# A bias row moved from TensorE's accumulation to GpSimd, in a three-layer graph attention kernel

## The reference

```
q = x @ Wq[k].T + bq[k];  kk = x @ Wk[k].T + bk[k]
scores = where(mask, -1e10, q @ kk.T / sqrt(128))
attn = where(mask, 0, softmax(scores))
ctx = (attn @ x) @ Wc[k].T
x = layer_norm(x + ctx, ln_g[k], ln_b[k])      # k = 0, 1
```

## Time and profile before

| | |
|---|---|
| median of 3 runs | 1202.79 us (1202.02 to 1202.92) |
| profiled execution, its own time | 1202.1 us |
| span of its trace | 1200.0 us, granted TensorE clock 0.989 of full |
| TensorE matmul busy | 1154.6 us (96%), 9596 matmuls |
| VectorE busy | 982.9 us (82%) |
| ScalarE busy | 928.5 us (77%) |
| GpSimd busy | 530.9 us (44%) |

### The profile page before, as it was taken

One profiled execution on the slowest core, in us unless ns is written; L12 is line 12 of the kernel. 1 busy time (PEld: TensorE's weight loads), 2 busy tenths in 40 slices (PEclk: granted clock), 3 DMA queues, 4 the chain that ended last, 5 costly groups with the idle time before them and its releaser, 6 DMA issues.

```text
span 1200.0 us, 28462 instructions
## 1 busy us (share of the span) xinstructions
PE 1154.6 (96%) x9596; PEld 843.5 (70%) x9596; DVE 982.9 (82%) x2688; ACT 928.5 (77%) x2115; POOL 530.9 (44%) x398
## 2 busy tenths in 40 slices
PE   7788999999999999999999999999999999999796
PEld 4566677777777777777777777777777777777463
DVE  5777788888888888888888888888888888988776
ACT  4426887888888788888878888887888888788774
POOL 1222445443564444356444534644453464444330
PEclk9898999999999999999999999999999999999999
DMA  8015160532517053251615325261432516122311
GB/s 228 19 36 141 20 190 24 148 81 73 140 37 194 19 141 90 72 141 36 180 33 136 89 72 148 36 179 34 127 89 80 148 36 180 34 71 72 111 32 36
DMA packets 164446, 112.48 MB, mean 94 GB/s; under 512 B 100944, under 2 KB 146000, under 8 KB 164304
## 3 DMA queue, kind: packets, MB, share of 16 engines
q1 hardware_dynamic: 162144, 102.80, 33.1%
q0 software_dynamic: 2160, 7.87, 1.9%
HBM read 61.87 MB, written 25.17 MB: 73 GB/s over the span
## 4 chain that ended last, share of the span: by engine, by line
PE 87%; DVE 6%; issue 2%; ACT 2%; DMA 2%; POOL 1%; DVEq 0%; SPq 0%; POOLq 0%; ACTq 0%
PE ps_j L848 39%; PE ps_t L861 22%; PE ps_j L988 9%; PE ps_s L840 8%; PE ps_s L834 6%; ACT probs L1048 1%; DMA xt<-ys 1%; DVE masked_s L1149 1%; PE ps_j L996 1%; POOL ys L674 1%; PE ps_j L955 0%; DVE wq L1199 0%; DVE y_l L1268 0%; DMA x<-x_dram 0%; DVE stats_L L1169 0%
## 5 line engine op out<-in xcount | busy, mean ns | idle before, releaser
L1149 DVE CUSTOM_DVE_ANT_0 masked_s<-ps_s,mask 128x512 f32<-128x512 f32 x640 | 424.6, 681 | 21.8 <-PE ps_s L840 20.7
L1048 ACT ACTIVATE probs<-masked_s,nm_h 128x512 f32<-128x512 f32 x512 | 367.3, 718 | 70.4 <-DVE nm_h L1149 63.9
L861 PE MATMUL ps_t<-ident,probs 128*128 128x128 f32 x2560 | 391.3, 276 | 5.6 <-ACT pt_h L1054 2.8
L861 PEld LDWEIGHTS ps_t<-ident,probs 128*128 128x128 f32 x2560 | 306.1, 142 | 85.5 <-issue 23.5
L1054 ACT ACTIVATE pt_h<-ps_t 128x512 f32<-128x512 f32 x401 | 236.2, 589 | 79.0 <-PE ps_t L861 74.3
L840 PE MATMUL ps_s<-stack 128*128 128x512 f16 x512 | 194.5, 380 | 2.6 <-DVE nm_h L1149 1.7
L848 PE MATMUL ps_j<-xw,pt_l 128*128 128x256 f16 x1536 | 189.1, 274 | 2.1 <-DVE xw L1294 2.1
L848 PEld LDWEIGHTS ps_j<-xw,pt_l 128*128 128x128 f16 x1536 | 151.0, 98 | 32.9 <-issue 2.2
L656 POOL TENSOR_TENSOR rstd_L<-var_eps_L,minus_half 128x4 f32<-128x4 f32 x32 | 32.8, 1024 | 246.5 <-DVE var_eps_L L1179 246.5
L988 PE MATMUL ps_j<-pt_h,v 128*32 128x256 f32 x2048 | 123.6, 382 | 2.4 <-DVE pt_h L1156 2.4
L1184 DVE TENSOR_TENSOR pt_l<-ps_t,pt_l 128x512 f16<-128x512 f32 x128 | 88.3, 690 | 32.5 <-ACT pt_l L1054 26.1
(11 more groups left out here) (140 smaller groups left out, 1639.4 us busy)
## 6 DMA issues: line engine op xcount, KB each, us to landing
stack<-bounce SPq DMA_DIRECT2D x256, 128.0 KB, 3.1
bounce<-parts SPq DMA_DIRECT2D x64, 256.0 KB, 2.6
adj_t<-adj_dram SPq DMA_DIRECT2D x30, 512.0 KB, 5.2
x<-x_dram SPq DMA_DIRECT2D x16, 512.0 KB, 3.9
out_dram<-y_f POOLq DMA_DIRECT2D x15, 512.0 KB, 3.4
stack<-adj_dram SPq DMA_DIRECT2D x2, 512.0 KB, 5.6
pt_h<-l_wc SPq DMA_DIRECT2D x2, 256.0 KB, 4.6
out_dram<-y_f SPq DMA_DIRECT2D x4, 128.0 KB, 1.8
```

The costliest lines, as they stand in the source:

```text
L861: last = pe.transpose(ps_t[r % 2][:, t], probs[:, r, t * P:(t + 1) * P], ident[:])
L1048: act.activation(probs[:, r], masked_s[:, r], ACT.Exp, bias=nm[:, n, r:r + 1], scale=-1.0, accum_out=total[:, n, r:r + 1]).then_inc(exps, 1)
L1149: dve.tensor_tensor_reduce(out=masked_s[:, r], in0=ps_s[scores_bank(pos)][:], in1=m[:, r], scale=-scale, scalar=NONE_LEFT, op0=ALU.add, op ...
```

## The change

The four bias matmuls of each graph's layer 1 XW job go, and with them `mean_64`. `bx1` is kept as one float32 row on all partitions. A new GpSimd function, `add_bx`, multiplies it by `has_l` (1 or 0 for each node) into a scratch tile (`y_l`, or `y_f` for graphs 0 and 1), four instructions of 128x256, and adds the tile to `x1`, one of 128x1024. VectorE gets one small reduction for each graph's layer 0, which makes `has_l` from the sums. GpSimd's order in a pass becomes `split_o(i, 1)`, `split_x(i+3)`, `add_bx(i+2)`, `finish(i)`, and the two M jobs go from tiles 29 and 32 to 33 and 34.

```diff
@@ LOOP_JOBS
-    ("M", None, "i+3", 0, (29,)),
-    ("M", None, "i+3", 1, (32,)),
+    ("M", None, "i+3", 0, (33,)),
+    ("M", None, "i+3", 1, (34,)),
@@ gpsimd
-                pool.tensor_tensor(dst[:], dst[:], h, ALU.add).then_inc(ln_done[s], 1)
+                pool.tensor_tensor(dst[:], dst[:], h, ALU.add).then_inc(shifted if norm == 0 else ln_done[s], 1)
...
+            def add_bx(b, dst):
+
+                if early(b, 1):
+                    pool.wait_ge(bias_ready, 1)
+                    settle(pool)
+                pool.wait_ge(shifted, b + 1)
+                spread = (y_f if early(b, 2) else y_l)[:]
+                for t in range(NT):
+                    last = pool.tensor_scalar(spread[:, t], bx1[:], zero[:], has_l[:, b % 2, t:t + 1], ALU.add, ALU.mult)
+                last.then_inc(bx_spread, 1)
+                pool.wait_ge(bx_spread, b + 1)
+                last = pool.tensor_tensor(dst[:], dst[:], spread, ALU.add)
+                last.then_inc(ln_done["L"], 1)
...
             layer_norm_l0(0, 0, x1)
+            add_bx(0, x1)
...
                 layer_norm_l0(i + 2, 0, x1)
+                split_o(i, 1)
                 split_x(i + 3)
-                split_o(i, 1)
+                add_bx(i + 2, x1)
                 finish(i)
@@ tensor, job XW
                     if early(b, 1) and l == 1:
-                        pe.wait_ge(bias_ready, 1)
                         pe.wait_ge(weights_ready, 2)
...
-                                             lambda a, c: wc0[:, a, l, c], more=l == 1)
-                        if l == 1:
-                            last = pe.matmul(out_bank[:, t * D:(t + 1) * D], mean_64[:], bx1[:],
-                                             start=False, stop=True)
+                                             lambda a, c: wc0[:, a, l, c])
@@ vector, job B
-                    dve.tensor_scalar(bx1[:], wide[:, 0:D], UP, None, ALU.mult).then_inc(bx1_hi, 1)
-                    dve.wait_ge(bx1_hi, 1)
-                    lower = slice(P // 2, P)
-                    dve.scalar_tensor_tensor(bx1[lower], wide[lower, 0:D], UP, bx1[lower], ALU.mult, ALU.subtract)\
-                        .then_inc(bias_ready, 1)
+                    dve.tensor_copy(bx1[:], wide[:, 0:D]).then_inc(bias_ready, 1)
@@ vector, job AV
+                        if l == 0:
+                            dve.tensor_reduce(has_l[:, b % 2], sum_l[:, sums_buffer(b, l), :, 0:3:2], ALONG, ALU.min)
-                        dve.tensor_reduce(some_l[:], sum_l[:, sums_buffer(b, l)], ALONG, ALU.max).then_inc(some_ready, 1)
+                        dve.tensor_reduce(some_l[:], sum_l[:, sums_buffer(b, l), :, 0:2], ALONG, ALU.max).then_inc(some_ready, 1)
```

More of the change, by code:

```diff
@@ L155, in graph_attention @@
         shift_c = sb("shift_c", [P, 2, DC])
-        bx1 = sb("bx1", [P, D], fp16)
-        mean_64 = sb("mean_64", [P, P], fp16)
+        bx1 = sb("bx1", [P, D])
         bv1 = sb("bv1", [P, D])
@@ L195, in graph_attention @@
         nm_h = sb("nm_h", [P, H, NT])
-        sum_l = sb("sum_l", [P, 2, NT, 2])
+        sum_l = sb("sum_l", [P, 2, NT, 3])
         sum_h = sb("sum_h", [P, H, NT])
         some_l = sb("some_l", [P, NT])
+        has_l = sb("has_l", [P, 2, NT])
+        zero = sb("zero", [P, 1])
         r_l = sb("r_l", [P, NT])
@@ L233, in graph_attention @@
         ident_zero, ident_in, half_in = sem("ident_zero"), sem("ident_in"), sem("half_in")
-        mean_in, bo_added, bx1_hi = sem("mean_in"), sem("bo_added"), sem("bx1_hi")
+        bo_added, shifted, bx_spread = sem("bo_added"), sem("shifted"), sem("bx_spread")
         pt_lo_ready, xw_hi = sem("pt_lo_ready"), sem("xw_hi")
@@ L645, in _ @@
             pool.memset(sum_l[:, :, :, 1:2], SUM_FLOOR).then_inc(floors_in, 1)
+            pool.memset(zero[:], 0.0).then_inc(floors_in, 1)
+            pool.memset(sum_l[:, :, :, 2:3], 1.0).then_inc(floors_in, 1)
             for s in "LF":
                 pool.memset(moments[s][:, :, 2:3], LN_EPS).then_inc(floors_in, 1)
-            pool.memset(mean_64[:], 1.0 / 64).then_inc(mean_in, 1)
             pool.wait_ge(ident_zero, 1)
@@ L760, in _ @@
             pool.tensor_tensor(x1[:], y_f[:], shift[:, 0:1, :].to_broadcast([P, NT, D]), ALU.add)\
-                .then_inc(ln_done["L"], 1)
+                .then_inc(shifted, 1)
+            add_bx(1, x1)
             pool.tensor_tensor(x2[:], y_l[:], gain[:, 1:2, :].to_broadcast([P, NT, D]), ALU.mult)\
@@ L781, in _ @@
             split_o(LOOPS - 1, 1)
+            add_bx(LOOPS + 1, x1)
             finish(LOOPS - 1)
@@ L1034, in _ @@
             pe.wait_ge(ident_in, 1)
-            pe.wait_ge(mean_in, 1)
             program(walk)
@@ L1301, in job @@
                         if early(L, 1):
-                            dve.wait_ge(floors_in, 3)
-                        dve.tensor_reduce(some_l[:], sum_l[:, sums_buffer(b, l)], ALONG, ALU.max).then_inc(some_ready, 1)
+                            dve.wait_ge(floors_in, 5)
+                        if l == 0:
+                            dve.tensor_reduce(has_l[:, b % 2], sum_l[:, sums_buffer(b, l), :, 0:3:2], ALONG, ALU.min)
+                        dve.tensor_reduce(some_l[:], sum_l[:, sums_buffer(b, l), :, 0:2], ALONG, ALU.max).then_inc(some_ready, 1)
                         dve.wait_ge(some_ready, L + 1)
```

## The result

The changed kernel is slower, by little: 1204.4 us in the median of 17 runs (1203.46 to 1206.31) against 1202.02 (1201.03 to 1204.07) for the kernel before, a ratio of 1.0019 (95% interval 1.0011 to 1.0026). I had forecast 1197.4 us and a range from 1195.4 to 1200.4.

The account below looks back on a forecast made before the run. TensorE was taken to bound the loop, and chains across engines the prologue. 6.2 us gained less 0.24 and 0.5 lost gave 5.4 us, so a median of 1197.4 us, range 1195.4 to 1200.4.

Parts of the forecast that it names:

- What bounds the kernel, and the price of the matmuls: Loop: TensorE bounds it, so four matmuls fewer save 0.44 us a pass, 6.2 us in 14 passes.
- The eight matmuls of the prologue: Prologue, graphs 0 and 1: removing them counts as nothing; at full price 0.9 us more.
- What comes on GpSimd: Loop: 4.6 us more GpSimd work a pass, ending 3.8 us before `finish` is due; cost nothing.
- The transfer: Loop: the transposing transfer behind `split_x(i+3)` is issued about 2.5 us later, with nothing waiting; cost nothing.
- The masks: Loop, VectorE: M moved behind a later mask tile costs 0, with bounds of 0 and some 0.2 us a pass.
- small waits: Rival, loop or prologue: TensorE waits 0.1 to 0.3 us a pass, or longer prologue; 1199 to 1201.5 us, chance 0.14.
- The prologue: Before the loop: 0.24 us lost to reductions and 0.5 us to VectorE's `wc` pieces.
- the `wc` pieces: Prologue: two VectorE instructions stand until GpSimd's new work ends at 56.8; 0.5 us, bounds 0 and 2.4.
- the two reductions: Prologue, VectorE: graphs 0 and 1 each pay for the new reduction, 0.12 us apiece, 0.24 us in all.
- Nothing comes of it: another chain is exactly as long: Rival, loop: the 0.44 us a pass turn into waits on another chain; 1202.8 us, chance 0.05.
- M is caught: Rival, loop: GpSimd's addition makes M stand 2.4 us; +1.3 us a pass, 1221 us with the prologue, chance 0.09.

Follow-up runs that it names:

- e10: Kernel before without the 64 bias matmuls, nothing in their place, and with the bank pair at tiles 30 and 32: 1196.08 us, ratio 0.9948.
- e11: Kernel before with the M jobs at tiles 33 and 34 and the bank pair at tiles 30 and 32: 1202.38 us, ratio 0.9999.
- e6: Kernel before without the bias matmuls, nothing in their place, and with the M jobs at 33 and 34: 1203.9 us, ratio 1.0014.
- e3: Kernel before with the 64 bias matmuls left out and nothing in their place: 1200.81 us, ratio 0.9994.
- e5: Changed kernel with the M jobs back at tiles 29 and 32, old score banks: 1225.68 us against the kernel before's 1202.02, ratio 1.0196.
- e9: Changed kernel with the bank pair at tiles 27 and 29 and the M jobs back at 29 and 32: 1214.58 us, ratio 1.0103 to the kernel before.
- e4: Kernel before with only the two M jobs moved from tiles 29 and 32 to 33 and 34: 1204.13 us, ratio 1.0016.

## Why the prediction was wrong, point by point

- **What bounds the kernel, and the price of the matmuls: right, as long as no mask is due.** e10's 6.2 us for 13 passes agree with my 0.44 us a pass, if anything with a little more. The eight matmuls of the prologue are worth nothing, as I had it: without them the two waits behind them, at 72 and 90 us, grow by what the matmuls took, from 2.11 to 2.56 us and from 2.03 to 2.47 (e11 against e10, both at the lower clock).
- **What comes on GpSimd: right.** The new instructions lie where I put them, to 0.2 us, and e6 shows that they cost nothing in the loop. The margin in front of the last norm was 4.27 us for a forecast of 3.8.
- **The transfer: right.** It starts 2.5 us later in the pass (532.02), and nothing waits for it.
- **The masks: here the step failed.** I wrote: "The sum of VectorE's work up to the mask tile at 608.29 is the same in either order." The work is the same, but VectorE's pauses are not, and the mask came 0.25 us later in most passes. But I took as the first thing due another one, "What is due next is XW's second half on VectorE", and worked out the slack of that, rightly: in the times of the earlier trace rows `xw` started at 609.85 (541.75 + 592.23 - 524.13), for a forecast of 609.6 to 609.9. The mask tile itself was due first. In the pass of the earlier trace rows it ended at 608.29 + 0.69 = 608.98 and TensorE's scores of tile 1 started at 609.18: 0.2 us to spare, of which a release takes 0.07 (541.22 to 541.29 above), so 0.13. "No pass shows such waits now", the prediction says of the small waits; two passes of the kernel before do, at this very place: the scores start 0.55 us behind the transposes at 679.27 and 0.67 behind those at 1030.63. The 0.44 us by which TensorE comes earlier use this up three times over, even if VectorE does nothing new, and e3 shows that alone. The prediction names no score bank: that `scores_bank` reuses one after two tiles at the seam of the pass stands nowhere in it. The cost, put at 0 with bounds of 0 and some 0.2 us a pass, was 0.56 us in each of 13 passes, 7.3 us; the bank pair alone moved gave 7.7 us back.
- **The prologue: size right by luck.** 0.74 us forecast, about 0.8 us on the mean of the profiles. But of the two terms neither is seen: the `wc` pieces, put at 0.5, have their old length in the changed kernel's profile (0.87 us), and the two reductions, put at 0.24 together, shift their neighbours by 0.06 to 0.07 each. What the 0.8 us consist of stays open.
- **The rivals.** "Nothing comes of it: another chain is exactly as long" was the right kind, at a chance of 0.05; I ruled it out by the slack of whole engines over a pass (over 11 us for each), and a sum over a pass says nothing on one tile. "M is caught" had the right mechanism and didn't happen, by luck as much as by working: M came 0.02 to 0.3 us behind GpSimd's addition. e5 and e9 show that it is real: with M in its old place it costs 21 us with the old banks and 17.5 with the new.
- With the term for the masks put right, my own sum, from the median of 17 runs before, is 1202.0 - 6.2 + 7.3 + 0.7 = 1203.8 us; 1204.4 was measured.

The version that beats both kernels is the change with the bank pair moved: 1196.77 us with the pair at 30 and 32, 1197.05 with it at 27 and 29, which is 0.9956 and 0.9958 of the kernel before; the change as it was is 1.0019.

## What to carry to other kernels

When the engine that bounds a loop gets shorter, look at every wait on it that now ends with little to spare, tile by tile, and take the distance of each buffer's reuse from the code, the seam of the loop included: a ring of 3 buffers in a loop of 40 steps has a place with distance 2. Put that place where the consumer is far ahead. A work share of 84% on another engine is no proof against a wait of half a microsecond at one tile.

## What the runs showed of the hardware

A VectorE mask (128x1024, int32 to bfloat16, SBUF to SBUF, 0.69 us alone) took 1.05 and 2.09 us when it met GpSimd's two-input instructions, and GpSimd's four 128x256 instructions took 2.60 instead of 2.16 us when they met the mask. The Trainium skill, SBUF — State Buffer, section "SBUF: two separate sides", says that the loser of the shared port pair stands for the rest of the other's instruction; these durations agree, in both directions: both masks end 0.55 us after GpSimd's instruction does (540.60 behind 540.05, 545.64 behind 545.09). A row of GpSimd instructions back to back didn't keep VectorE out for good: the first mask of e5 got in between two of them. In the prologue the clock granted to TensorE between 70 and 80 us was 0.83 in three profiles and 0.66 or 0.67 in ten, and e4 and e11, which run the same instructions there but for the banks, are on different sides. 48 matmuls took 7.07 us at 0.83 and 8.11 at 0.66 in these two, yet their first marks lie only 0.11 us apart (159.58 and 159.69).
